# A two-block kernel on one core: first chunk prepared inside the preparation, and VectorE's normalisation of the network's next chunk spread over more tiles

## The reference

```python
# block 0
shift_a, scale_a, gate_a, shift_ff, scale_ff, gate_ff = jnp.split(t @ Wm + bm, 6, axis=-1)
y_mod = _ln(y) * (1 + scale_a[:, None]) + shift_a[:, None]
a_y = _s5(y_mod, ...)     # complex diagonal recurrence over the rows: B_bar u, scan, C, and D * u
y = y + gate_a[:, None] * a_y
scale_c, shift_c = jnp.split(t @ Wc + bc, 2, axis=-1)
y_norm = _ln(y) * (1 + scale_c[:, None]) + shift_c[:, None]
y_mod = y_norm * (1 + scale_ff[:, None]) + shift_ff[:, None]
y = y + gate_ff[:, None] * (gelu(y_mod @ W1 + b1) @ W2 + b2)
# block 1: layer norm with gamma, beta = t @ Wg.T + bg, t @ Wb.T + bb; attention of 16 heads;
# projection; the same layer norm again
```

## Time and profile before

| | |
|---|---|
| median of 3 runs | 2956.81 us (2954.97 to 2958.14) |
| the profiled execution | 2956.91 us, of which the span of the trace is 2955.1 us |
| PE busy | 2852.5 us, 97% of the span |
| DVE busy | 1988.9 us, 67% |
| POOL busy | 1814.4 us, 61% |
| ACT busy | 1525.2 us, 52% |
| HBM read and written | 144.51 MB and 92.31 MB |

### The profile page before, as it was taken

The page is one execution under the profiler, slowest core; times in us unless marked ns, Lnnn a source line. Parts: engine busy times, 40 slices in busy tenths (PEclk is TensorE's granted clock), DMA queues, the critical chain, the costliest instruction groups (busy, mean ns, idle before and its releaser), DMA issues.

```text
span 2955.1 us, 40978 instructions
## 1 busy us (share of the span) xinstructions
PE 2852.5 (97%) x14818; PEld 1916.9 (65%) x14818; DVE 1988.9 (67%) x3534; ACT 1525.2 (52%) x2788; POOL 1814.4 (61%) x840
## 2 busy tenths in 40 slices
PE   4899999999999999999999999999999999999997
PEld 2787788888888887755555555555555555555456
DVE  7873332322323555768888888888888888888539
ACT  3552232332333321246676667666666667666744
POOL 2676310111100333238999899999899999999854
PEclk8899999999999999999999999999999999999999
DMA  6443100000001567486779887788877789777868
GB/s 217 164 147 123 58 15 15 29 29 29 29 0 62 184 214 220 173 201 137 165 155 192 189 183 158 163 177 192 190 154 165 168 194 190 170 150 163 188 194 300
DMA packets 158650, 431.84 MB, mean 146 GB/s; under 512 B 12501, under 2 KB 30905, under 8 KB 134742
## 3 DMA queue, kind: packets, MB, share of 16 engines
q0 software_dynamic: 26208, 190.85, 32.8%
q1 hardware_dynamic: 132248, 238.41, 25.2%
HBM read 144.51 MB, written 92.31 MB: 80 GB/s over the span
## 4 chain that ended last, share of the span: by engine, by line
DMA 22%; POOL 16%; PE 11%; issue 6%; DVE 1%; ACT 0%; POOLq 0%; DVEq 0%; SPq 0%; ACTq 0%
DMA pair<-pair 13%; POOL pair L2007 9%; DMA pair<-raw_weight 5%; DMA raw_weight<-pair 4%; PE psum L1759 3%; PE psum L1771 3%; PE psum L1744 2%; POOL raw_weight L2007 2%; POOL pair L2002 2%; POOL pair L1984 1%; POOL v_out L1970 1%; PE psum L37 1%; PE psum L39 1%; PE psum L38 1%; PE psum L1799 1%
## 5 line engine op out<-in xcount | busy, mean ns | idle before, releaser
L1890 DVE TENSOR_REDUCE part_max<-psum 128x1 f32<-128x512 f32 x1984 | 1211.7, 679 | 165.5 <-PE psum L1744 160.0
L1856 ACT ACTIVATE probs<-psum 128x512 f32<-128x512 f32 x2048 | 1042.3, 614 | 448.0 <-PE psum L1759 446.2
L1759 PE MATMUL psum<-queries,keys 128*128 128x512 f32 x2048 | 838.6, 412 | 7.8 <-PEq L2403 3.1
L2007 POOL TENSOR_TENSOR pair<-probs 128x2048 f32<-128x2048 f32 x163 | 767.8, 4717 | 85.4 <-ACT probs L1856 83.3
L1744 PE MATMUL psum<-keys,queries 128*128 128x512 f32 x1984 | 788.3, 398 | 0.5
L1759 PEld LDWEIGHTS psum<-queries,keys 128*128 128x128 f32 x2048 | 383.7, 188 | 342.7 <-issue 214.5
L1771 PE MATMUL psum<-probs,values 128*32 128x512 f32 x4096 | 507.0, 600 | 0.0
L1081 DVE TENSOR_TENSOR h_lo<-w_stage,h_hi 128x512 fp32r<-128x512 f32 x128 | 101.0, 790 | 484.3 <-ACT h_hi L989 484.2
L1744 PEld LDWEIGHTS psum<-keys,queries 128*128 128x128 f32 x1984 | 373.6, 188 | 76.2 <-DVE part_max L1890 23.8
L982 ACT ACTIVATE w_stage<-psum,b_col 128x512 f32<-128x512 f32 x128 | 88.3, 690 | 481.7 <-PE psum L39 480.9
L1771 PEld LDWEIGHTS psum<-probs,values 128*32 128x32 f32 x4096 | 107.1, 109 | 241.7 <-ACT probs L1856 125.7
(11 more groups left out here) (346 smaller groups left out, 4075.1 us busy)
## 6 DMA issues: line engine op xcount, KB each, us to landing
pair<-pair POOLq DMA_DIRECT2D x113, 1024.0 KB, 8.1
pair<-raw_weight POOLq DMA_DIRECT2D x35, 1024.0 KB, 8.1
raw_weight<-pair POOLq DMA_DIRECT2D x34, 1024.0 KB, 7.9
queries<-q_parts SPq DMA_DIRECT2D x96, 256.0 KB, 4.0
keys<-k_parts SPq DMA_DIRECT2D x42, 512.0 KB, 7.9
s_x<-in_x_dram SPq DMA_DIRECT2D x8, 1024.0 KB, 8.1
s_y<-in_x_dram SPq DMA_DIRECT2D x8, 1024.0 KB, 5.4
y_rows<-s_y SPq DMA_DIRECT2D x8, 1024.0 KB, 4.7
```

Source lines behind the costliest of these rows:

```text
L1759: nc.tensor.matmul(psum[:, SC + unit % 3, :], keys[place(count)[0]][:, h, kt * P:(kt + 1) * P], queries[count % NQ][:, h, :], start=True, ...
L1856: act.activation(probs[tile % NPROB][:, h, :], psum[:, SC + unit % 3, :], ACT.Exp).then_inc(exp_ready, 1)
L1890: dve.tensor_reduce(part_max[:, h * TT + qt, kc:kc + 1], max_slot(), AX.X, ALU.max).then_inc(max_read, 1)
L2007: pool.tensor_tensor(target[:, :, :], even[:, :, :], odd[:, :, :], ALU.add).then_inc(pair_ready, 1)
```

## The change

In the preparation: the loads come in another order (SP): the first chunk `x[0]` and the matrices `C` after four of the six tiles of `wm`, `wc` last. The groups of projections become (0 to 3), (8, 9), (4 to 7). The bias is added by one more small matmul of `mod` in the same PSUM sum, and ACT writes each result straight to `vec` or `mod` (`take_row`); POOL's additions are gone. The work on chunks 0 and 1 that stood at the start of the state-space stage stands in the preparation: the moments and inverse of both on DVE, the normalisation, transposes, `u`, `u_hi` and `u_lo` of chunk 0, the gate load, and `cg_ready`, the product of `C` with the gate. So the state-space stage starts with `gate_outputs` without that product, and with chunk 0 ready.

In the network: DVE's statistics of the next chunk stay before tile 8, the small moment work goes before tile 9, the inverse before tile 11, and the normalisation is cut in two halves, two row groups before tile 12 and two before tile 13. `norm_ready` counts row groups.

```diff
@@ prep_stage, VectorE @@
+            moments(0)
+            invert(0)
             for n in range(2):
-                dve.wait_ge(bc_hi, 3 + n)
+                dve.wait_ge(b_hi, n + 1)
...
+            moments(1)
+            invert(1)
...
+            dve.wait_ge(rows_copied, 6)
+            link(dve.tensor_tensor(vec[:, V_GAIN_1, :], mod[:, 8, :], ln_gb[:, 0, :], ALU.mult))
...
+            dve.wait_ge(gate_ld, 16 * B)
+            dve.wait_ge(c_copied, 2)
+            for b in range(B):
+                for n in range(2):
+                    dve.tensor_tensor(prod[:, 2 * b + n, :], s5["c"][:, n, :], gate[b][:, :], ALU.mult).then_inc(cg_ready, 1)
+            dve.wait_ge(rows_copied, 10)
...
@@ prep_stage, ScalarE @@
+            def take_row(group, n, out, plus):
+
+                act.wait_ge(sec_ready, group + 1)
+                act.activation(out, projection(group, n), ACT.Identity, bias=plus).then_inc(rows_copied, 1)
...
@@ prep_stage, TensorE @@
+                pe.wait_ge(ld_row, 16 * 6 * B)
+                for n in GROUPS[group]:
+                    mm = pe.matmul(projection(group, n), ident[0:B, 0:B], mod[:, n, :], start=False, stop=True)
+                mm.then_inc(sec_ready, 1)
...
@@ s5_stage, VectorE @@
         def gate_outputs():
-            dve.wait_ge(gate_ld, 16 * B)
             for b in range(B):
-                for n in range(2):
-                    dve.tensor_tensor(prod[:, 2 * b + n, :], s5["c"][:, n, :], gate[b][:, :], ALU.mult).then_inc(cg_ready, 1)
                 dve.tensor_tensor(d_gated[:, b, :], s5["d"][:, :], columns[:, V_GATE_A, :, b], ALU.mult).then_inc(dg_ready, 1)
...
-        moments(0)
-        invert(0)
-        moments(1)
-        invert(1)
         gate_outputs()
...
@@ ffn_stage, VectorE @@
                 if j == LN_TILE and nxt:
+                    tile_statistics(*nxt)
+                if j == LN_TILE + 1 and nxt:
                     moments(*nxt)
-                if j == LN_TILE + 2 and nxt:
-                    normalise(*nxt)
+                if j == LN_TILE + 3 and nxt:
+                    invert(*nxt)
+                if j == LN_TILE + 4 and nxt:
+                    normalise(*nxt, range(0, TT // 2))
+                if j == LN_TILE + 5 and nxt:
+                    normalise(*nxt, range(TT // 2, TT))
```

More of the change, by code:

```diff
@@ L111, in prep_stage @@
     pow2 = sb("prep_pow2", [P, 1], I32)
-    ld_ssm, ld_cond, ld_row, ld_wc, ld_wgb = (sem(f"prep_ld_{n}") for n in ("ssm", "cond", "row", "wc", "wgb"))
-    ld_wm = [sem(f"prep_ld_wm{n}") for n in range(3)]
+    u, u_hi, u_lo, norm, prod, gate = (s5[n] for n in ("u", "u_hi0", "u_lo0", "norm", "prod", "gate"))
+    c_in = [u[n][:, :].rearrange("d (k q) -> d k q", q=P) for n in range(2)]
+    stats, moment = s5["stats"], s5["moment"]
+    var, root, rough, square, inv, off = (s5[n] for n in ("var", "root", "rough", "square", "inv", "off"))
@@ L120, in prep_stage @@
     chain = sem("prep_chain")
[L121 to L130, removed]
+    bbar_ready, c_tp, b_tp, c_copied, b_hi, b_lo = (sem(n) for n in ("bbar_ready", "c_tp", "b_tp", "c_copied", "prep_b_hi", "prep_b_lo"))
@@ L169, in _ @@
                                pattern=[[-1, P]], channel_multiplier=1).then_inc(ident_ready, 1)
[L171 to L174, removed]
+            for k in range(KT):
+                pool.wait_ge(u_ready, 2 * (k + 1))
+                pool.tensor_tensor(u_lo[:, k, :], u[k % 2][:, :], u_hi[:, k, :].bitcast(F32), ALU.subtract).then_inc(ulo_ready, 1)
@@ new lines, in take_root, with take_columns @@
+            def take_root(c):
+                act.wait_ge(var_ready, c + 1)
+                act.activation(root[:, :], var[:, :], ACT.Sqrt).then_inc(root_ready, 1)
+            def take_columns(first, last):
+                at = [COLS + v * KT * B for v in (first, last + 1)]
+                act.activation(columns[:, first:last + 1, :, :], psum[:, SMALL, at[0]:at[1]].rearrange("p (v k b) -> p v k b", k=KT, b=B),
+                               ACT.Copy).then_inc(col_ready, 1)
+            act.wait_ge(cond_tp, 1)
@@ new lines, in _ @@
+            take_root(0)
+            for n, times in enumerate((2.0, -2.0)):
+                act.wait_ge(c_tp, n + 1)
+                act.activation(s5["c"][:, n, :], psum[:, TURNED + n, :], ACT.Copy, scale=times).then_inc(c_copied, 1)
+            act.wait_ge(inverse, INVERSE)
+            for t in range(TT):
+                act.activation(norm[:, t, :], x[0][:, t, :], ACT.Identity, scale=inv[:, t:t + 1], bias=off[:, t:t + 1]).then_inc(norm_ready, 1)
+            act.wait_ge(col_tp, 1)
+            take_columns(V_GAIN_A, V_SHIFT_A)
@@ L2358, in cond_seq_kernel @@
                 own("s5_pad", [P, OPERAND_STEP - 3 * HD])
+                s5["u"] = [own(f"u{n}", [P, CH]) for n in range(2)]
+                for part in ("hi", "lo"):
+                    s5[f"u_{part}0"] = own(f"u_{part}0", [P, KT, CH], F32R)
+                s5["prod"] = own("prod", [P, 4, CH])
+                s5.update({"norm": ahead["norm"], "gate": ahead["gate"], "x": x, "y_first": y_first, "raw_weight": raw_weight})
+                s5["gate_ld"], s5["x_ld"] = sem("s5_gate_ld"), [sem(f"s5_x_ld{b}") for b in range(B)]
+                s5.update({n: sem(f"s5_{n}") for n in ("stat", "aggregated", "var_ready", "root_ready", "inverse",
+                                                       "norm_ready", "tr_ready", "u_ready", "ulo_ready", "cg_ready")})
                 with ExitStack() as stage:
```

313 lines of the change are left out of this document (184 added, 129 removed).

## The result

| | before | changed kernel |
|---|---|---|
| median of 5 runs | 2956.88 us (2954.97 to 2958.14) | 2940.85 us (2933.15 to 2947.12) |
| the profiled execution | 2956.91 us, span 2955.1 | 2942.97 us, span 2941.2 |

The ratio is 0.9948, with a 95% interval of 0.9937 to 0.9959: faster by 16.0 us, where 16.7 were forecast. The forecast of 2940.2 was met, but not by its own sum: the start won 4 to 5 us more than I had it, and TensorE gave 7.3 us back at a place that the prediction does not name. The changed kernel's five runs spread over 14 us and those of before over 3 us, but that is no mark of the change: later sets of runs of the kernel before spread over 9 to 12 us, and of the changed kernel over 7.

What follows compares the result with a forecast made beforehand. A serial stretch before attention bounds the kernel, with TensorE bounding the steady stages, so only its time without input can be won: 2956.9 - 9.5 (start) - 7.2 (network) = 2940.2 us, own range 2937.5 to 2943.

Steps and rivals of the forecast that it cites:

- What bounds the kernel: Everything before attention is one serial stretch; a microsecond saved there moves attention by a microsecond.
- The start: Preparation and state-space start: stage begins 3.3 us later, first `prod` at 76.1 instead of 85.57; gain 9.5 us, bounds 4 to 13.5.
- The vectors were ready: End of preparation: vectors ready, last transposes starting, at 59.7 us, where it was 56.4.
- the 3.7 that I carried over from before: From vectors ready to the state-space stage's start: 3.7 us kept, from 56.4 to 60.1 before.
- the 12.25 us from 73.32 to 85.57: VectorE's work ahead of the first `prod` in the state-space stage, taken to stay at 12.25 us.
- four hold-ups: Doubling loop in the preparation: GpSimd still holds up four VectorE instructions, so 14.7 us kept, 10.7 without such waits.
- The network: First chunk: TensorE's stall for `h_lo`, costing 7.46 us, goes except 0.3; gain 7.2 us, nothing in the other seven chunks.
- The preparation did not grow: Rival, chance 0.2: hand-overs or slow TensorE lengthen the preparation; 4 to 7 of the 9.5 us gone, 2944 to 2947.
- the stall did not move: Rival, chance 0.13: TensorE stops at `h_lo` of tile 11 instead; 2 to 4 of 7.2 us remain, 2943.5 to 2945.5.
- the gate's load: Sign of being wrong: in the preparation the gate's load is the last thing VectorE waits for.
- The engines meet at 1265.7: Sign of being right: all engines meet before attention at 1265.7 us, not 1282.4.
- A change in attention's length: Sign of being wrong: attention, which the change does not touch, takes a different time.

Runs made afterwards that it cites:

- the run with GpSimd beside it: Changed kernel with two more products of 128x512 on GpSimd, results unused, at the start of the state-space stage: 2944.58 us, one run.
- the reordered one: Changed kernel with its preparation in another order (decay and first doubling earlier, projections 4 to 7 before 8 and 9): 2940.74 us, again 2940.14 us.
- the padding of 48: Changed kernel with 48 tiny unused transposes on TensorE in the preparation: 2943.20 us, again 2941.88 us.
- that of 16: Changed kernel with 16 tiny unused transposes on TensorE in the preparation: 2934.54 us, ratio 0.9921.

## Why the prediction was right, point by point

**What bounds the kernel** held: what was won ahead of attention arrived there, 16.1 us of it.

**The start: 9.5 us forecast, 13.6 measured.** The order of events was as described, each mis-sized in the same direction. The vectors were ready at 58.6, not 59.7, since the doubling loop began and ended 1.1 us sooner than forecast. The end of the block took 2.8 us from there, not the 3.7 that I carried over from before. And the step "the 12.25 us from 73.32 to 85.57" stay failed by 2.1 us: I took the part behind the vectors as unchanged, and did not ask who had been at work beside it. GpSimd's `u_lo` had been moved away from it; the run with GpSimd beside it brought 1.9 us of the 2.1 back. The same thing was priced correctly in the doubling loop, where I kept four hold-ups (decay and loop 15.8 us forecast, 15.8 measured, 36.12 to 51.90; one of the four fell on the decay), and in the network. In the state-space stage another 1.1 us came to it; nothing shows that it belongs to the change, since from the first `prod` to the network's first statistics the profiled executions took 201 to 205 us. The same goes for 1.5 us in `qkv_stage`, which took 302 to 306 us.

**The network: 7.2 us forecast, 7.3 measured** with the network's part alone. Spreading divides the hold-ups and does not remove them: four of the inverse's six instructions still take 1.0 to 1.2 us, but nobody waits for them. The other seven chunks cost nothing, 89.3 us per chunk in both.

**What the sum left out** is the turns. TensorE's list grew by 41 entries in the preparation, by my count, and I counted each at its duration there and none for what it does to the loop 350 us later: 7.3 us, the size of the network's whole gain. So 13.6 + 1.1 + 7.3 - 7.3 is 14.7 at the end of the network, where 16.7 was forecast. None of the rivals describes this.

**The rivals.** The preparation did not grow, the stall did not move (no wait for `h_lo` in the first chunk, where 0.3 us were allowed), and the gate's load held nobody in the changed kernel; it did in the reordered one, for 0.5 and 0.6 us. "The engines meet at 1265.7" came out at 1266.6, by errors of both signs. A change in attention's length was named as a sign of being wrong, and attention is 2 us longer in the profile; with a range of 14 us among executions that says nothing about the change.

## What to carry to other kernels

A change that only adds instructions ahead of a loop can cost or win at every turn of that loop, far from where it was made. Look in the new profile for "issue" at the first matmuls of a round, and for packets on the queue of instructions; if a loop is near the size of what stays on the chip, try it with a few useless instructions ahead of it before judging the change itself. In this kernel that was worth 6.3 us of 2941, and 10.6 us the other way; at the turns themselves the traces show 7.4 and 4.8 of them. Measure it, too: the padding of 48 removed the same stands as that of 16, and its median lay at the changed kernel's.

When an engine's work is moved, price also what it held up where it was: each of GpSimd's products of 128x512 cost VectorE about 1 us where small instructions stood beside it.

And do the parts of a change alone. The total of 16.0 us looked like the forecast's 16.7, and only the stage by stage difference showed two errors that cancelled.

## What the runs showed of the hardware that was not expected

At the turn of a loop in TensorE's list, with a packet of 16 KB of instructions 0.27 us behind the first matmul of the new round: TensorE stood for 1.5 to 2.3 us when it wanted those instructions after two or three matmuls, and not at all when it wanted them some 20 matmuls later. Padding of 16 or 48 transposes, 32 or 96 entries, removed 18 packets from the whole execution (121 to 103 on q8).

A stand of 1.5 to 2.3 us cost 2.4 to 4.9 us, by the length of the round (178.7 us without a stand), and two things behind it go with the difference over the 14 turns in seven executions: whether the granted clock falls, and whether `h_lo` is late by 0.6 us or more. With neither it was 2.4 to 2.5 us (seven turns), with the clock alone 3.7 to 3.9 (three), with `h_lo` alone 3.7 (one), with both 4.9 (three).

The start of attention has a stand of its own in TensorE, of 1.8 to 5.2 us, 3.9 and 5.2 with the padding of 48 and at most 2.7 elsewhere; its cause was not settled.
